# Softmax attention in a hybrid block: the value matmuls of two key tiles issued as one group

## The reference, cut to what matters

```python
qkv = x @ w_qkv                      # x normalised; q and k rotated
scores = einsum('bhqd,bhkd->bhqk', q, k) / sqrt(8)
probs = softmax(scores, axis=-1)
out = einsum('bhqk,bhkd->bhqd', probs, v)
return out @ w_out + b_out
```

## Time and profile before

| | |
|---|---|
| median of 3 runs | 5906.45 us (5892.85 to 5911.36) |
| the profiled execution, own time | 5901.95 us |
| its span | 5900.1 us |
| mean granted TensorE clock | 0.955 of full |
| busy, whole span | PE 87%, DVE 75%, ACT 65%, POOL 50% |
| 250 to 900 us (650 us) | PE 605.98, PEld 193.45, DVE 504.55, ACT 443.61, POOL 37.79 us busy; clock 0.99 |
| 950 to 995 us (45 us) | PE 42.58, DVE 3.65, ACT 39.56 us busy; clock 1.00 |

### The profile page before, as it was taken

The page is one execution under the profiler, slowest core; times in us unless marked ns, Lnnn a source line. Parts: engine busy times, 40 slices in busy tenths (PEclk is TensorE's granted clock), DMA queues, the critical chain, the costliest instruction groups (busy, mean ns, idle before and its releaser), DMA issues. The chain is left out here.

```text
span 5900.1 us, 135041 instructions
## 1 busy us (share of the span) xinstructions
PE 5113.0 (87%) x38884; PEld 3411.9 (58%) x38884; DVE 4421.2 (75%) x8097; ACT 3864.6 (65%) x11648; POOL 2938.9 (50%) x2878
## 2 busy tenths in 40 slices
PE   5999997898988989989889677989989889898897
PEld 1223222566666666666666455666666666666665
DVE  7777775786876868868778546868868778687785
ACT  1666665775776757757667405757757677577675
POOL 3000000665665656656566306656656566566564
PEclk6999999999999999999999868999999999999999
DMA  0000001212222221121221202122222221212223
GB/s 12 1 1 1 1 1 38 60 48 70 52 58 58 52 70 47 48 73 48 68 54 47 75 9 82 48 69 53 60 57 49 69 52 47 73 49 60 59 51 85
DMA packets 332293, 288.23 MB, mean 49 GB/s; under 512 B 149102, under 2 KB 290708, under 8 KB 329748
## 3 DMA queue, kind: packets, MB, share of 16 engines
q1 hardware_dynamic: 331028, 282.33, 18.6%
q10 hardware_dynamic: 768, 0.02, 0.0%
HBM read 100.81 MB, written 30.41 MB: 22 GB/s over the span
## 5 line engine op out<-in xcount | busy, mean ns | idle before, releaser
L416 DVE TENSOR_REDUCE a_maxima<-a_max 128x1 f32<-128x512 f32 x1024 | 652.2, 686 | 195.8 <-PE a_max L530 191.8
L985 ACT ACTIVATE g_ex<-g_bank,g_nmx 128x96 f32<-128x96 f32 x1536 | 501.4, 338 | 345.3 <-DVE g_nmx L1067 345.3
L985 ACT ACTIVATE f_ex<-f_bank,f_nmx 128x96 f32<-128x96 f32 x1536 | 501.4, 338 | 343.1 <-DVE f_nmx L1067 343.1
L340 ACT ACTIVATE a_pex<-a_scores 128x1024 f32<-128x1024 f32 x512 | 517.1, 1026 | 217.4 <-PE a_scores L539 208.7
L920 POOL TENSOR_TENSOR f_rn<-f_sg,f_minus_half 128x8 f32<-128x8 f32 x384 | 640.1, 1667 | 32.0
L920 POOL TENSOR_TENSOR g_rn<-g_sg,g_minus_half 128x8 f32<-128x8 f32 x384 | 639.7, 1666 | 32.0
L925 POOL TENSOR_TENSOR f_qr<-f_t 128x512 f32<-128x512 f32 x384 | 547.7, 1426 | 14.8 <-DVE f_t L1086 13.1
L925 POOL TENSOR_TENSOR g_qr<-g_t 128x512 f32<-128x512 f32 x384 | 537.2, 1399 | 14.8 <-DVE g_t L1086 13.1
L1162 PE MATMUL g_bank<-g_wqkv,g_xT 128*128 128x512 f32 x768 | 427.7, 640 | 87.2 <-DVE g_qh L1077 62.1
L1162 PE MATMUL f_bank<-f_wqkv,f_xT 128*128 128x512 f32 x768 | 427.5, 639 | 86.6 <-DVE f_qh L1077 61.7
L530 PE MATMUL a_max<-a_stackT 128*128 128x512 bf16 x1024 | 410.9, 402 | 57.1 <-DVE a_maxima L416 26.2
(11 more groups left out here) (235 smaller groups left out, 13205.3 us busy)
## 6 DMA issues: line engine op xcount, KB each, us to landing
f_vw<-f_vt SPq DMA_DIRECT2D x96, 384.0 KB, 4.3
g_vw<-g_vt SPq DMA_DIRECT2D x96, 384.0 KB, 4.3
f_vw<-f_vt SPq DMA_DIRECT2D x96, 256.0 KB, 3.6
g_vw<-g_vt SPq DMA_DIRECT2D x96, 256.0 KB, 3.6
f_vw<-f_vt SPq DMA_DIRECT2D x96, 128.0 KB, 2.3
g_vw<-g_vt SPq DMA_DIRECT2D x96, 128.0 KB, 2.3
f_wqkv<-in_f_Wqkv_dram SPq DMA_DIRECT2D x7, 1536.0 KB, 7.3
g_wqkv<-in_f_Wqkv_dram SPq DMA_DIRECT2D x7, 1536.0 KB, 9.4
```

The costliest lines, as they stand in the source:

```text
L340: act.activation(pex[:, kt % 2, 2 * j:2 * j + 2, :], ps_s[j][:], ACT.Exp).then_inc(act_ex, 1)
L416: dve.tensor_reduce(maxima[:, m // 4, m % 4:m % 4 + 1], ps_max[m % 2][:], AX.X, ALU.max).then_inc(dv_max, 1)
L985: last = act.activation(ex[:, b, u, :], ps_s[:, KEYS * u:KEYS * u + KEYS], ACT.Exp, bias=nmx[:, b, u:u + 1], accum_out=sm[:, b, u:u + 1])
```

## The change

The ring of exponentials grows from two key tiles to four. The value matmuls of two key tiles (16 records) are issued one right after the other at steps 5, 9, 13, ... 29, and for the last two key tiles at step 1 of the next head; steps 3, 7, 11, ... 31 have none. The number of matmuls, their shapes and their operands stay as they are. The semaphore pe_pv starts at 4, and those who wait for it count from there.

```diff
-        pex = sb("pex", [P, 2, NG, GQ])
+        pex = sb("pex", [P, 4, NG, GQ])
@@ gpsimd, head
-                    pool.wait_ge(pe_pv, NT * h + 2).then_inc(own["pool"], 1)
+                    pool.wait_ge(pe_pv, NT * h + 4).then_inc(own["pool"], 1)
@@ scalar, head
-                    act.activation(pex[:, kt % 2, 2 * j:2 * j + 2, :], ps_s[j][:], ACT.Exp).then_inc(act_ex, 1)
+                    act.activation(pex[:, kt % 4, 2 * j:2 * j + 2, :], ps_s[j][:], ACT.Exp).then_inc(act_ex, 1)
@@ vector, sums
-                dve.wait_ge(pe_pv, NT * h + (NT + 2))
+                dve.wait_ge(pe_pv, NT * h + (NT + 4))
@@ tensor
-            pe.sem_inc(pe_pv, 2)
+            pe.sem_inc(pe_pv, 4)
@@ tensor, values
-                    last = pe.matmul(ps_o[VW * g:VW * g + VW, :], v_head[:, p, kt, :], pex[:, kt % 2, g, :],
+                    last = pe.matmul(ps_o[VW * g:VW * g + VW, :], v_head[:, p, kt, :], pex[:, kt % 4, g, :],
@@ tensor, head
-                    if n > 1 and n % 2:
+                    if n > 1 and n % 4 == 1:
+                        values(h, u % 2, n // 2 - 2)
                         values(h, u % 2, n // 2 - 1)
                     elif n == 1 and exists(h, -1):
+                        values(h - 1, (u + 1) % 2, NT - 2)
                         values(h - 1, (u + 1) % 2, NT - 1)
@@ tensor, after all heads
+            values(HEADS - 1, 1, NT - 2)
             values(HEADS - 1, 1, NT - 1)
```

## The result

The changed kernel takes 5924.05 us (median of 17 runs, 5917.76 to 5933.25) against 5910.48 before (17 runs, 5892.85 to 5917.73): ratio 1.0024, 95% interval 1.0017 to 1.0032, so 14 us slower. The forecast stood on three runs before, with a median of 5906.45. In a later job it was 5920.34 against 5902.28, ratio 1.0035 (1.0023 to 1.0048). The profiled execution has 5926.36 us of its own and a span of 5924.5.

What follows compares the result with a forecast made beforehand. The prediction saw a chain across TensorE and VectorE taking turns, value blocks exposed beyond two reductions. Terms 17.3 - 0.2 + 4.2 + 7.4 + 0.9 made +29.6 us; forecast 5933 us, range 5915 to 5950.

Steps and rivals of the forecast that it cites:

- eight intervals of a head: Softmax stage, stretches between value groups from steps 1 to 5 through 29 to 1: together +1.33 us for a head.
- a wash: Rival: double group near 1.85, outputs find cover, heads without maxima stall less; +5 to +17 us, chance 0.12.
- A reduction at 0.63, four at 2.53: VectorE's pace without value matmuls: 0.63 us a maximum; four extra reductions before the next wait add 2.53 us.
- A double group at 1.90: TensorE's joined value matmuls of two key tiles: 1.00 plus 0.90 for two more passes, range 0.85 to 1.00.
- Outputs uncovered at step 6: Steps 5 to 9: VectorE's outputs lose the idle time of step 7's value group; 0.61 us exposed, interval +0.89.
- Transposes alone nearly covered, negated maxima covered: Steps 17 to 21 and 21 to 25: -0.10 each; steps 25 to 29, maxima under the longer block: -0.44.
- Steps 29 to 1: End of a head, second transposes waiting for ScalarE's copy of the first: 7.28 to 7.49 us, +0.21.
- Heads 14 and 15: Last heads, maxima partly or wholly gone: ScalarE stalls, 5.09 for 4.17 us per four steps; +4.2 and +7.4.
- Jumps of the loop: At two jumps, at half clock, a double group pays 0 to 0.9 us more each; +0.9 for both.
- The turns of the array: TensorE loses 0.18 us entering and leaving each value group; the change makes half as many such turns.
- my rival: TensorE is the bound and saved turns gain 23 us, if a double group costs under 1.61 us; chance 0.06.

Runs made afterwards that it cites:

- the kernel with short value matmuls: Kernel before with 16 columns in place of 512 in all value matmuls but those of key tile 0; 5756.83 us, ratio 0.9754.

## Why the prediction was right, and where its sizes were off

The direction and the mechanism came out: all eight intervals of a head are within 0.15 us of the forecast and have its sign, though steps 29 to 1 and not 5 to 9 are the longest. The size was about twice the measured one: +29.6 for +15.7 in the stage and +14 in the medians. That is a change which the rival "a wash" had (+5 to +17), and short of the 18 us above which I had put 0.82 of the chances. The time itself, 5924.05, lies in the range partly by luck: the median before came out 4 us higher than on three runs, and the range reached down to the upper part of the wash. Of the wash's conditions one held, the double group near 1.85; outputs found no cover, and the heads without maxima stalled as forecast. In the heads with maxima, up to head 14's turned sums, my terms make 19.2 us and the trace 6.7; behind them they make 10.4 and the trace 9.0. Nearly the whole error is in the first part:

- *A reduction at 0.63, four at 2.53.* This term was mis-sized. In the earlier trace rows the 2.53 holds a short wait and a tail: b's matmul ends 0.61 after a's reduction starts, and b's reduction can start only at 0.65; the last record lasts 0.68. Once matmuls are ahead, reductions follow each other by 0.60 to 0.61 (2.42 for four in the kernel with short value matmuls; eight in 4.96 after the change). That is about 0.10 less in each of the eight intervals.
- *A double group at 1.90.* Mis-sized too. It is 1.86: the second pass starts 0.45 after the first, the third and fourth 0.43 after the one before. Again 0.04 in each interval. Both together are 0.14, 1.1 us a head; a wait that I left out (below) takes 0.28 of it back, and the 0.82 that stay make 11.5 us over 14 heads, most of the 14 between forecast and stage. (The pairs are 128, not 127; this changes nothing.) They look small beside a pair of 6.4, but the price of the change is the difference of two near-equal sums, +0.29 forecast and +0.16 found.
- *Outputs uncovered at step 6.* Right: +0.77 for the +0.89 forecast, and all but 0.16 of it came back when they were moved.
- *Transposes alone nearly covered, negated maxima covered.* Right: -0.25 and -0.57 for -0.10 and -0.44, off by the same 0.14. The reduction behind the negated maxima follows them by 0.04, not by 0.17.
- *Steps 29 to 1.* Too low, 7.49 for 7.63, though the two terms above should have made it too high. I left out a wait: the next head's first maximum matmul stands behind the head's entry wait for the second copy. The rows of the changed kernel:

```profile
748.34 1.02 ACT L333 COPY a_stackT<-a_turned 128x1024 bf16<-128x1024 bf16 x1
...
749.48 0.39 PE L530 MATMUL a_max<-a_stackT 128*128 128x512 bf16 x1 [0.42 <-ACT a_stackT L333]
```

  VectorE would have let it start at 749.20, so the wait costs 0.28. Before, a value group stood there, and the copy (743.92 and 1.02 long) had ended 0.63 before the next maximum matmul (745.57).
- *Heads 14 and 15.* From head 14's turned sums on, the trace has +9.0 us; my terms give 10.4. At 5.03 for two key tiles against my 5.09 the mechanism is shown by its trace and by the kernel with single groups there.
- *Jumps of the loop.* +0.3 for +0.9, and +0.5 in the second trace of the changed kernel. As the jumps of the other kernels spread far more, this term is within the noise.
- *The turns of the array.* They do cost something: two groups apart hold the array for 2 x 1.00, together for 1.86, so 0.14 us for one way in and out. The Trainium skill, "TensorEngine Tiling (Array Packing)", Key Properties, says that a change of tiling mode drains the engine, and the trace agrees as far as there is a gap; its size is from these rows. By that rule alone the change would have won 18 us. The 0.14 was won, and is part of the 1.86. But each single block has a cover of its own, 0.28 by the short value matmuls, and two blocks joined have it only once: 0.28 - 0.14 = +0.14 for a plain pair, +0.16 found. So the point from which a double group pays is 1.72 us (1.00 + 0.72), not the 1.61 of my rival.

The rise of 24 us between the two profiled executions is not all of the change: 9 us lie behind the stage, in code that is the same in both, and the medians don't show them. In the traces of all kernels here that rest takes between 4898 and 4919 us.

## What to carry to other kernels

When two engines pass small buffers to and fro, ask how much of a block on one engine the work in hand on the other covers, before you join or split blocks. Here three stretches of TensorE's other work between two maximum matmuls, of different length, each had a cover of nearly 0.3 us. By the intervals, less 0.605 us a reduction:

| other work in one stretch | us | cost beyond VectorE's pace |
|---|---|---|
| value block | 1.00 | 0.72 |
| value block and transposes | 1.45 | 1.17 |
| double block | 1.86 | 1.60 |

What goes beyond the cover is paid for, and two pieces in one stretch share a single cover. Setting pieces of different kinds apart, with no work removed, brought 34 to 36 us, while halving the number of blocks by doubling their length lost 14, 9 of them where only exponentials were left to cover them. Look as well at what lay in the idle time that goes away, and take the pace of a chain from a stretch where nothing else waits, not from a busy time that holds a wait.

## What the runs showed that I had not expected

- Reductions of 128 x 512 last 0.686 us each by their mean, but follow each other by 0.605: records overlap, and the count times the mean overstates the time of a full queue by about 13%.
- Four passes of the value matmuls in a row: 0.45 to the second, 0.43 to each further one. The records of a group's first pass last 0.617 us and those of later passes 0.592, in both kernels; a double group has more of the later ones, so the median falls from 0.616 to 0.592:

```profile
L549 PE MATMUL a_sums<-a_pex,a_v_head x1492: 592/592/1059, 249.4 to 897.0; 128*32 128x512 f32 x187
```
